# Odd heads of pairs 9 to 14: queries and keys from 7 block products in place of 8

## The chip, the cores and the metric

The kernel runs on one core of a Trainium2 chip. The metric is device time in microseconds (us) of one launch; the median of three runs of the kernel before is 1061.95 us.

## The reference, cut to what matters

```python
def _L0_attn_ref(hidden_states, Wq, bq, Wk, bk, Wv, bv, Wo, bo, gq, gk):
    q = hidden_states @ Wq + bq
    k = hidden_states @ Wk + bk
    v = hidden_states @ Wv + bv
    q = rms_norm(q, gq)
    k = rms_norm(k, gk)
    attn = softmax(q @ k.T / sqrt(128)) per head
    return (attn @ v) @ Wo + bo

x = x + _layernorm(_L0_attn_ref(_layernorm(x), ...))
x = x + _layernorm(_L0_ffn_ref(_layernorm(x), ...))
```

The input is 2 batches of 512 tokens, 512 wide; there are 32 heads of 128. The norm of queries and keys runs over all heads (4096 columns), so every query and key must be known before the first score.

## The kernel before, in words

Every float32 product is made of three float16 matmuls: each operand is split into a high half and a low half, and high x high, high x low and low x high are summed in PSUM (`three`, L1619). A stationary operand is 128x128, the moving one 512 columns.

**Phase A** (to about 330 us) computes queries and keys, head by head in 16 pairs of an even and an odd head (heads 2p and 2p+1 are pair p). TensorE's part is `q_or_k` (L1663): for a head four products, query and key (w = 0, 1) of batch 0 and of batch 1, each of 4 chunks x 3 = 12 matmuls of 512 columns. So a head is 48 matmuls. The even head writes PSUM banks 0 to 3, the odd one banks 4 to 7. The other engines' parts for a head:

- ScalarE (`phase_a`, L1198): the high halves of the weights of the head after next (`high_wa`), then per product the square (`square`, L1149, into `squares`), and for a query two copies with bias, the float32 one `q_s` (L1159) and its high half (L1161).
- GpSimd (`phase_a`, L762): for each batch the low half of the query (`low_q`, L747) and two additions of the squares to `acc` (`add_batch`, L753). After each head comes one more step, `more(par)`, which forms operands for block products of values: sums and differences of blocks of x, split into halves in `xs` (`high_a` to `split_g`, L796 to L837), 36 instructions in pairs 1 to 13 (L868 to L881).
- VectorE (`phase_a`, L2382): scale factors of the head after next (`next_factors`), its largest weight four heads ahead (`largest_qk`), the low halves of the weights (`low_wa`, L2219, two instructions of 512 columns with both tensors in SBUF), the key with bias and gain (`store_k`, L2324), and a reduction of one unit of the value or output weights (`largest_of_unit`).
- SyncE loads weights five heads ahead and stores query and key to DRAM.

Each engine's order is written out by hand; semaphores with running counts hold it together. In phase A TensorE waits for the low halves of the weights (`wa_lo_ready`) and for the key before in the same banks (`k_out_ready`), L1699 to L1710.

**Phase B** computes scores, softmax, values and outputs, pair by pair. Values of most pairs are already made there by the block scheme with 7 products (`product`, L1809), with the operands `xs` that GpSimd formed in phase A; SyncE waits for all 36 forms before it loads over their scratch `qk_in` (L577).

## Time and profile before

| what | us |
|---|---|
| runs | 1060.37, 1062.02, 1061.95 (median 1061.95) |
| the profiled execution, its own time | 1060.19 |
| its span | 1058.4 |
| TensorE busy | 1039.7 (98%) |
| VectorE busy | 828.2 (78%) |
| ScalarE busy | 764.0 (72%) |
| GpSimd busy | 763.4 (72%) |
| mean granted TensorE clock | 0.998 |

Busy time is what an engine spent in instructions, without the time in which it waited for a semaphore. 1.8 us of the profiled execution lie outside its span. A share over the whole span says little of phase A, whose third of the time has other loads than the rest; so the rows below are of stretches.

### The profile page before, as it was taken

What the parts mean: (1) busy time and instruction counts of PE and PEld (TensorE: products, weight loads), DVE (VectorE), ACT (ScalarE), POOL (GpSimd) and SP (SyncE); (2) the same over time, 40 slices, a digit from 0 to 9 for tenths busy, and PEclk for the clock granted to TensorE, in tenths of its full rate; (3) what the DMA queues carried; (4) which work ended last, traced back from release to release, by engine and by line L of the source; (5) the groups of instructions that cost most, each with busy time, mean ns of one, the idle gap of its engine ahead of it and who ended that gap; (6) DMA issues with size and microseconds to landing.
All of it is one profiled execution on the core that took longest, in us unless ns stands there. A gap on an engine that the chain in (4) does not pass through costs nothing.

```text
span 1058.4 us, 19677 instructions
## 1 busy us (share of the span) xinstructions
PE 1039.7 (98%) x5649; PEld 549.8 (52%) x5649; DVE 828.2 (78%) x1824; ACT 764.0 (72%) x1582; POOL 763.4 (72%) x717
## 2 busy tenths in 40 slices
PE   7999999999999999999999999999999999999997
PEld 4444444444444655556555555555555555555454
DVE  7777876667646778777887987888888888878887
ACT  4666766666647777776788787778787878877756
POOL 2687988788958577765777777778778778767313
PEclk9999999999999999999999999999999999999999
DMA  6678865656574569967667867876877987896702
GB/s 242 176 235 269 254 231 210 227 195 233 201 139 164 178 175 262 250 160 197 149 170 185 195 166 172 200 187 157 203 197 143 216 203 161 224 198 141 177 34 81
DMA packets 312761, 199.91 MB, mean 189 GB/s; under 512 B 275552, under 2 KB 279520, under 8 KB 312672
## 3 DMA queue, kind: packets, MB, share of 16 engines
q1 hardware_dynamic: 304752, 194.24, 68.1%
q10 hardware_dynamic: 7920, 4.62, 1.7%
q8 instruction: 39, 0.64, 0.2%
q14 instruction: 50, 0.41, 0.1%
HBM read 96.03 MB, written 35.68 MB: 124 GB/s over the span
## 4 chain that ended last, share of the span: by engine, by line
PE 87%; DVE 6%; ACT 3%; issue 1%; DMA 1%; POOL 1%; SPq 0%; DVEq 0%; ACTq 0%; POOLq 0%
PE ps L1621 26%; PE ps L1623 25%; PE ps L1622 25%; PE ps L1813 3%; PE ps L1814 3%; PE ps L1815 3%; ACT ps L1301 2%; DVE pair_q L2542 1%; ACT pair_q L1310 1%; DVE y L2555 1%; DMA pair_k<-pair_q 1%; DMA wa_stage<-w_qk 1%; DVE ps L2528 1%; DVE stats L2117 0%; PE ps L1733 0%
## 5 line engine op out<-in xcount | busy, mean ns | idle before, releaser
L1301 ACT ACTIVATE ps<-ps,neg_max 128x512 f32<-128x512 f32 x256 | 168.2, 657 | 57.7 <-DVE ps L2528 57.7
L2542 DVE SCALAR_TENSOR_TENSOR pair_q<-ps,row_inv,pair_q 128x512 f16<-128x512 f32 x256 | 174.2, 742 | 43.8 <-ACT pair_q L1310 40.4
L1621 PE MATMUL ps<-xh,wa_hi 128*128 128x512 f16 x512 | 194.1, 379 | 1.8 <-DVE wa_lo L2222 1.8
L1622 PE MATMUL ps<-xl,wa_hi 128*128 128x512 f16 x512 | 194.1, 379 | 0.0
L1623 PE MATMUL ps<-xh,wa_lo 128*128 128x512 f16 x512 | 194.1, 379 | 0.0
L2528 DVE TENSOR_SCALAR_CACHE_REDUCE ps<-ps,score_down 128x512 f32<-128x512 f32 x256 | 177.1, 753 | 15.2 <-PE ps L1623 14.5
L1310 ACT ACTIVATE pair_q<-ps,row_inv 128x512 f16<-128x512 f32 x256 | 154.5, 689 | 9.0 <-DVE row_inv L2535 8.8
L759 POOL TENSOR_TENSOR acc<-acc,squares 128x512 f32<-128x512 f32 x120 | 151.5, 1284 | 1.6 <-ACT squares L1152 1.6
L1152 ACT ACTIVATE squares<-ps,q_k_bias,qk_down 128x512 f32<-128x512 f32 x128 | 99.1, 785 | 42.9 <-PE ps L1623 28.6
L750 POOL TENSOR_TENSOR qk_out<-q_s,qk_out 128x512 f16<-128x512 f32 x64 | 75.5, 1181 | 52.4 <-ACT qk_out L1161 52.4
L2327 DVE TENSOR_SCALAR qk_out<-ps,k_b,k_g 128x512 f32<-128x512 f32 x64 | 51.8, 809 | 73.9 <-ACT squares L1152 73.8
L905 POOL TENSOR_TENSOR k_lo<-qk_in,k_hi 128x512 f16<-128x512 f32 x62 | 71.7, 1157 | 38.2 <-ACT k_hi L1258 38.1
L1621 PE MATMUL ps<-wo_hi,oth 128*128 128x512 f16 x256 | 97.1, 379 | 1.9 <-issue 0.9
L1621 PE MATMUL ps<-k_hi,qk_in 128*128 128x512 f16 x256 | 97.1, 379 | 1.2 <-issue 0.9
L1623 PE MATMUL ps<-wo_hi,otl 128*128 128x512 f16 x256 | 97.1, 379 | 0.0
L1622 PE MATMUL ps<-wo_lo,oth 128*128 128x512 f16 x256 | 97.1, 379 | 0.0
L1623 PE MATMUL ps<-k_hi,qk_in 128*128 128x512 f16 x256 | 97.1, 379 | 0.0
L1622 PE MATMUL ps<-k_lo,qk_in 128*128 128x512 f16 x256 | 97.0, 379 | 0.0
L1119 ACT ACTIVATE wa_hi<-wa_stage,qk_up 128x512 f16<-128x512 f32 x64 | 42.8, 718 | 75.0 <-DVE qk_up L2174 75.0
L936 POOL CAST oth<-o_t 128x512 f16<-128x512 f32 x62 | 38.3, 618 | 74.0 <-ACT o_t L1275 73.9
L1275 ACT ACTIVATE o_t<-ps,tab 128x512 f32<-128x512 f32 x62 | 42.7, 689 | 58.8 <-PE ps L1623 58.7
L1621 PEld LDWEIGHTS ps<-xh,wa_hi 128*128 128x128 f16 x512 | 50.3, 98 | 61.9 <-issue 2.1
(310 smaller groups left out, 2578.3 us busy)
## 6 DMA issues: line engine op xcount, KB each, us to landing
q_k_scratch<-qk_out SPq DMA_DIRECT2D x64, 512.0 KB, 4.0
qk_in<-q_k_scratch SPq DMA_DIRECT2D x64, 512.0 KB, 3.7
wa_stage<-w_qk SPq DMA_DIRECT2D x32, 512.0 KB, 4.2
u_stage<-w_vo SPq DMA_DIRECT2D x32, 512.0 KB, 5.3
wo_stage<-w_vo SPq DMA_DIRECT2D x16, 512.0 KB, 6.3
x_first<-w_vo SPq DMA_DIRECT2D x12, 512.0 KB, 4.4
qk_tops<-qk_top_scratch ACTq DMA_DIRECT2D x27, 128.0 KB, 3.5
pair_k<-pair_q SPq DMA_TRANSPOSE x130, 4.0
```

The lines of the kernel that those rows point to most:

```text
L750: pool.tensor_tensor(pair(qk_out[:, par, b, 1, :])[:, 1, :], q_s[:, par, b * S:(b + 1) * S], pair(qk_out[:, par, b, 1, :])[:, 0, :], ALU.s ...
L759: pool.tensor_tensor(acc[:, w, cols], acc[:, w, cols], squares[:, par, w, cols], ALU.add).then_inc(acc_ready, 1)
L905: pool.tensor_tensor(k_lo[:, s % 2, :], qk_in[:, s, 0, :], k_hi[:, s % 2, :], ALU.subtract).then_inc(qk_lo_ready, 1)
L1152: act.activation(squares[:, par, w, b * S:(b + 1) * S], ps[:, 4 * par + g, :], ACT.Square, bias=q_k_bias[:, par, w:w + 1], scale=qk_down[: ...
L1301: act.activation(ps[:, SCORE + i, :], ps[:, SCORE + i, :], ACT.Exp, bias=neg_max[:, sl, i:i + 1], scale=-1.0, accum_out=row_sum[:, sl, i:i ...
L1310: act.activation(pair_q[:, 0, i, :], ps[:, SCORE + i, :], ACT.Identity, scale=row_inv[:, sl, i:i + 1]).then_inc(high_ready, 1)
L1621: pe.matmul(outp, lhs[0], rhs[0], start=first, stop=False)
L1622: pe.matmul(outp, lhs[0], rhs[1], start=False, stop=False)
L1623: return pe.matmul(outp, lhs[1], rhs[0], start=False, stop=last)
L2327: dve.tensor_scalar(qk_out[:, par, b, 0, :], ps[:, 4 * par + 2 * b + 1, :], k_b[:, slot:slot + 1], k_g[:, slot:slot + 1], ALU.add, ALU.mul ...
L2528: dve.tensor_scalar(ps[:, SCORE + i, :], ps[:, SCORE + i, :], score_down[:, sl, i:i + 1], None, ALU.mult, ALU.min, accum_out=neg_max[:, sl ...
L2542: dve.scalar_tensor_tensor(out=pair_q[:, 1, i, :], in0=ps[:, SCORE + i, :], scalar=row_inv[:, sl, i:i + 1], in1=pair_q[:, 0, i, :], op0=AL ...
```

## The change

For six pairs (9 to 14) the odd head's query and key are no longer four products of 12 matmuls. Tokens are split into the first and the second 256 of each batch, the contraction into its first and last two chunks, the output into query and key: a product of 2x2 blocks, done with 7 block products (C, A, E, B, D, G, F) of 2 chunks x 3 = 6 matmuls of 512 columns. Four of the sums that the scheme wants are made by leaving products in PSUM and copying bank to bank.

- TensorE (`formed_pair`): the even head's four `q_or_k` with the odd head's block products between them, 90 matmuls for the pair. Before A it waits, in the first formed pair, for all forms of x (`x_formed` 30), in the others for the sums of queries before.
- GpSimd: the forms of x now stand in pairs 1 to 8, two after most heads (30 instructions). `formed_sums` adds and subtracts blocks of the next formed head's weights into `f_sum` (one instruction of 512 columns, three of 256), once between pairs 7 and 8 and then in pairs 9 to 13 after two additions. The low halves and additions of the odd head go by tokens.
- VectorE: forms the sums of G (six instructions `half_g` and `both_g`, in heads 7 to 12), adds saved C to the query banks (two instructions of 512 columns for a formed head), and splits the formed weights in `low_formed`: 512 columns that are used as they are and 1280 of sums.
- ScalarE: saves C with its bias, copies bank to bank three times for a formed head, squares the odd head's query from SBUF; `high_formed` has one instruction of 512 and one of 1280 columns.
- Both factors of a formed head become one (`next_factors(..., formed=True)`), since query and key weights are added.
- The pairs from 9 on are straight code on all engines; SyncE stores the odd head's two batches together at the pair's end.

Cut to its core:

```diff
@@ gpsimd
+            def formed_sums(h):
+                slot, f = h % 4, h // 2 - FIRST
+                pool.wait_ge(wa_loaded[slot], 16 * (h // 4 + 1))
+                if f > 0:
+                    pool.wait_ge(wa_lo_ready, 2 * h - 2)
+                w = wa_stage[:, slot]
+                pool.tensor_tensor(f_sum[:, 0:4 * P].rearrange("p (w c n) -> p w c n", w=2, c=2), w[:, :, 0:2, :],
+                                   w[:, :, 2:4, :], ALU.add).then_inc(w_formed, 1)
+                for k, one, other, op in ((F_E, w[:, 0, 0:2, :], w[:, 1, 2:4, :], ALU.add),
...
+                low_q(0, 0, 2 * h + 1)
+                add_one(1, -1, 0, 0, batch(0))
+                add_one(2, 0, 0, 1, batch(0))
+                if p < LAST_PAIR:
+                    formed_sums(h + 3)
+                add_one(3, 2, 1, 1, tokens(0))
...
-            phase_a(1, high_a)
-            phase_a(2, low_a)
-            phase_a(3, both_halves)
-            phase_a(4, split_a)
...
+            phase_a(1, high_a, low_a)
+            phase_a(2, both_halves, half(high_half, XA))
+            phase_a(3, half(low_half, XA), high_e)
+            phase_a(4, low_e, half(high_half, XE))
+            phase_a(5, half(low_half, XE), high_d)
+            phase_a(6, low_d, half(high_half, XD))
+            phase_a(7, half(low_half, XD), high_half_g)
+            formed_sums(2 * FIRST + 1)
+            phase_a(8, low_half_g)
+            for p in range(FIRST, LAST_PAIR + 1):
+                formed_pair(p)
@@ scalar
+            def high_formed(h):
+                slot, f = h % 4, h // 2 - FIRST
+                act.wait_ge(qk_up_ready, h + 1)
+                act.activation(corners(wa_hi[:, slot]), corners(wa_stage[:, slot]), ACT.Copy,
+                               scale=qk_up[:, slot, 0:1]).then_inc(wa_hi_ready, 1)
+                act.wait_ge(w_formed, 4 * f + 4)
+                act.activation(f_high[f % 2], f_sum, ACT.Copy,
+                               scale=qk_up[:, slot, 0:1]).then_inc(wa_hi_ready, 1)
@@ tensor
-            with pe.Fori(1, PAIRS // 2) as i:
+            with pe.Fori(1, PAIRS // 4 + 1) as i:
...
+                q_or_k(0, 0, slots[0])
+                pe.wait_ge(wa_lo_ready, 2 * h + 4)
+                pe.wait_ge(k_out_ready, 2 * h - 1)
+                product(W_C, C_BANK, True)
+                if f:
+                    pe.wait_ge(q_sum_ready, 2 * f)
+                else:
+                    pe.wait_ge(x_formed, X_FORMS)
+                product(W_A, Q_LAST, True)
+                q_or_k(0, 1, slots[0])
+                pe.wait_ge(v_copied, 4 * f + 2)
+                product(W_E, Q_LAST, False)
+                product(W_B, K_BANK, False)
+                q_or_k(0, 2, slots[0])
+                pe.wait_ge(v_copied, 4 * f + 3)
+                product(W_D, Q_LAST, False)
+                product(W_G, Q_FIRST, False)
+                q_or_k(0, 3, slots[0])
+                pe.wait_ge(v_copied, 4 * f + 4)
+                product(W_F, K_BANK, False)
@@ vector
+                dve.wait_ge(qk_product, products + 9)
+                for second, bank in enumerate((Q_FIRST, Q_LAST)):
+                    dve.wait_ge(v_copied, 4 * f + 3 + second)
+                    dve.scalar_tensor_tensor(out=over_tokens(q_s[:, 1, :], second), in0=by_half(ps[:, bank, :]),
+                                             scalar=Q_DOWN, in1=by_half(c_q), op0=ALU.mult,
+                                             op1=ALU.add).then_inc(q_sum_ready, 1)
+                if p < LAST_PAIR:
+                    low_formed(h + 3)
+                else:
+                    low_wa(h + 3, (h + 3) % 4)
+                dve.wait_ge(stored[0][1], 16 * p)
+                store_k(0, 1, slots[0], 8 * p + 6)
+                formed_key(1, 8 * p + 8)
```

How it moves instructions, at the two places that matter below. First GpSimd, from the odd head of pair 7 to the first formed pair. Before, the end of pair 7 and pair 8 (L750 is the low half of a query, L759 an addition of squares, L776 and L793 form and split x):

```order
L776 TENSOR_TENSOR xs<-qk_in,xs 128x512
L750 TENSOR_TENSOR qk_out<-q_s,qk_out 128x512
L759 TENSOR_TENSOR acc<-acc,squares 128x512 x2
L750 TENSOR_TENSOR qk_out<-q_s,qk_out 128x512
L759 TENSOR_TENSOR acc<-acc,squares 128x512 x2
L776 TENSOR_TENSOR qk_in<-xh,qk_in 128x512
```

Now the same place (L815 and L824 are the low half and the additions, L841 and L858 the forms of x, L902 and L907 the sums of weights):

```order
L841 TENSOR_TENSOR xs<-qk_in,xs 128x512
L858 CAST xs<-qk_in 128x512
L902 TENSOR_TENSOR w_sum<-wa_stage 128x512
L907 TENSOR_TENSOR w_sum<-wa_stage 128x256 x3
L815 TENSOR_TENSOR qk_out<-q_s,qk_out 128x512
L824 TENSOR_TENSOR acc<-acc,squares 128x512 x2
L815 TENSOR_TENSOR qk_out<-q_s,qk_out 128x512
L824 TENSOR_TENSOR acc<-acc,squares 128x512 x2
L841 TENSOR_TENSOR xs<-qk_in,xs 128x512
```

The sums of weights stand ahead of pair 8, and the last split of x, the one TensorE waits for, stands behind all of pair 8's additions.

Second VectorE, at the end of a formed pair (with the semaphores that each instruction waits for; L2748 adds C to the queries, L2495 and L2499 split the next formed head's weights, L2603 and L2725 write keys):

```order
L2748 SCALAR_TENSOR_TENSOR q_s<-ps,k_lo 128x2x256 [waits v_copied,qk_product]
L2748 SCALAR_TENSOR_TENSOR q_s<-ps,k_lo 128x2x256 [waits v_copied]
L2495 SCALAR_TENSOR_TENSOR wa_lo<-wa_stage,qk_up,wa_hi 128x2x256 [waits wa_hi_ready]
L2499 SCALAR_TENSOR_TENSOR rms_row<-w_sum,qk_up,rms_row 128x1280 [waits wa_hi_ready]
L2603 TENSOR_SCALAR qk_out<-ps,k_b,k_g 128x512 [waits sq_ready,stored0_1]
L2725 TENSOR_SCALAR qk_out<-ps,k_b,k_g 128x2x256 [waits sq_ready]
```

Both keys that end the pair now stand behind the split of 1280 columns, whose input comes from GpSimd by way of ScalarE. TensorE, at the start of the next pair, waits for them and for that split:

```order
L1820 MATMUL ps<-xh,wa_lo 128x512
L1939 MATMUL ps<-xh,w_form_a 128x512 [waits k_out_ready,wa_lo_ready]
L1940 MATMUL ps<-xl,w_form_a 128x512
L1941 MATMUL ps<-xh,w_form_a 128x512
L1939 MATMUL ps<-xh,w_form_a 128x512
L1940 MATMUL ps<-xl,w_form_a 128x512
L1941 MATMUL ps<-xh,w_form_a 128x512
L1939 MATMUL ps<-xs,wa_hi 128x512 [waits x_formed]
```

C (six matmuls) comes 12 matmuls into the pair, and in the first formed pair A stands 18 matmuls in, behind the wait for the forms of x.

## Rows read from the trace of the kernel before

**Rows 1.** The page: busy time, and slices of the span (tenths).
```profile
PE 1039.7 (98%) x5649; PEld 549.8 (52%) x5649; DVE 828.2 (78%) x1824; ACT 764.0 (72%) x1582; POOL 763.4 (72%) x717
PE   7999999999999999999999999999999999999997
POOL 2687988788958577765777777778778778767313
```

**Rows 2.** Windows in phase A: us, busy of each engine (instructions), PEclk, DMA share, GB/s.
```profile
100.00:140.00 40.00, 40.00 (x187) 18.16 (x186) 32.02 (x59) 28.47 (x49) 38.38 (x31) 1.00 0.84 273
225.00:245.00 20.00, 20.00 (x94) 9.10 (x93) 13.69 (x28) 13.01 (x22) 16.45 (x16) 1.00 0.57 208
```

**Rows 3.** Timeline, TensorE at 238 us: start us, us, instruction.
```profile
238.16 0.38 PE L1621 MATMUL ps<-xh,wa_hi 128*128 128x512 f16 x1
238.38 0.38 PE L1622 MATMUL ps<-xl,wa_hi 128*128 128x512 f16 x1
```

**Rows 4.** Timeline, ScalarE: squares that wait for a head's last product.
```profile
204.70 0.78 ACT L1152 ACTIVATE squares<-ps,q_k_bias,qk_down 128x512 f32<-128x512 f32 x1 [0.66 <-PE ps L1623]
...
215.06 0.78 ACT L1152 ACTIVATE squares<-ps,q_k_bias,qk_down 128x512 f32<-128x512 f32 x1 [0.66 <-PE ps L1623]
```

**Rows 5.** Timeline, GpSimd, heads 5 to 11, with idle time before and releaser.
```profile
81.40 1.16 POOL L750 TENSOR_TENSOR qk_out<-q_s,qk_out 128x512 f16<-128x512 f32 x1 [2.60 <-ACT qk_out L1161]
...
101.41 1.16 POOL L750 TENSOR_TENSOR qk_out<-q_s,qk_out 128x512 f16<-128x512 f32 x1 [1.56 <-ACT qk_out L1161]
102.52 2.49 POOL L759 TENSOR_TENSOR acc<-acc,squares 128x512 f32<-128x512 f32 x2
104.98 1.16 POOL L750 TENSOR_TENSOR qk_out<-q_s,qk_out 128x512 f16<-128x512 f32 x1
...
108.55 1.72 POOL L776 TENSOR_TENSOR qk_in<-qk_in 128x512 f32<-128x512 f32 x1
110.32 1.51 POOL L750 TENSOR_TENSOR qk_out<-q_s,qk_out 128x512 f16<-128x512 f32 x1
...
117.80 1.08 POOL L793 CAST xs<-qk_in 128x512 f16<-128x512 f32 x1
118.96 1.48 POOL L776 TENSOR_TENSOR xs<-qk_in,xs 128x512 f16<-128x512 f32 x1
120.40 1.16 POOL L750 TENSOR_TENSOR qk_out<-q_s,qk_out 128x512 f16<-128x512 f32 x1
...
130.16 1.16 POOL L750 TENSOR_TENSOR qk_out<-q_s,qk_out 128x512 f16<-128x512 f32 x1
...
138.88 1.61 POOL L750 TENSOR_TENSOR qk_out<-q_s,qk_out 128x512 f16<-128x512 f32 x1
```

**Rows 6.** Timeline, GpSimd, head 17.
```profile
200.95 1.16 POOL L750 TENSOR_TENSOR qk_out<-q_s,qk_out 128x512 f16<-128x512 f32 x1 [1.99 <-ACT qk_out L1161]
...
208.08 1.17 POOL L776 TENSOR_TENSOR qk_in<-xh,qk_in 128x512 f32<-128x512 f16 x1
```

**Rows 7.** Timeline, VectorE: the two splits of weights of one head.
```profile
108.06 2.76 DVE L2222 SCALAR_TENSOR_TENSOR wa_lo<-wa_stage,qk_up,wa_hi 128x512 f16<-128x512 f32 x2
```

**Rows 8.** By tile and by source: durations in ns, min/median/max.
```profile
L2222 DVE SCALAR_TENSOR_TENSOR wa_lo<-wa_stage,qk_up,wa_hi x64: 736/746/1754, 13.2 to 328.1; 128x512 f16<-128x512 f32 x64
L2542 DVE SCALAR_TENSOR_TENSOR pair_q<-ps,row_inv,pair_q x256: 732/741/752, 355.9 to 998.6; 128x512 f16<-128x512 f32 x128
```

**Rows 9.** Groups of GpSimd, 140 to 200 us: busy us, mean ns, idle before.
```profile
L750 POOL TENSOR_TENSOR qk_out<-q_s,qk_out 128x512 f16<-128x512 f32 x12 | 14.3, 1193 | 8.5 <-ACT qk_out L1161 8.5
L776 POOL TENSOR_TENSOR xs<-qk_in,xs 128x512 f16<-128x512 f32 x2 | 2.3, 1154 | 0.2
L793 POOL CAST xs<-qk_in 128x512 f16<-128x512 f32 x2 | 1.2, 616 | 0.0
```

**Rows 10.** Timeline, TensorE: first matmuls of constants, and the last matmul.
```profile
1.76 5.30 PE L1634 MATMUL ps<-ones,ident 128*128 128x256 f16 x24 [1.76 <-POOL ident L727]
...
10.84 1.47 PE L1634 MATMUL ps<-ones,ident 128*128 128x256 f16 x12
...
1050.83 0.27 PE L1623 MATMUL ps<-bt_hi,hw_lo 128*128 128x256 f16 x1
```

**Rows 11.** Windows behind the last matmul, columns as in rows 2.
```profile
1052.00:1054.00 2.00, 0.00 (x0) 0.00 (x0) 1.93 (x4) 0.11 (x1) 2.00 (x2) 1.00 0.10 38
1054.00:1056.00 2.00, 0.00 (x0) 0.00 (x0) 1.84 (x5) 0.00 (x0) 0.61 (x2) 0.72 0.95 355
1056.00:1058.40 2.40, 0.00 (x0) 0.00 (x0) 0.00 (x0) 0.00 (x0) 0.00 (x0) 0.50 0.29 109
```

**Rows 12.** Waits, 100 to 325 us: us in total, times, longest.
```profile
DVE qk_most L2207 <- DMA qk_tops<-qk_top_scratch: 8.4, 2, 7.4
```

396 lines of the change are left out of this document (312 added, 84 removed).

## The prediction

> **What bounds the kernel now.** Read the page's busy times first [rows 1]: TensorE is busy in 98% of the span and in nine tenths or more of every slice but the first and the last. The windows of phase A say the same in its middle, 20.00 of 20.00 us at full clock, while VectorE, ScalarE and GpSimd have a fifth to a third of their time free there [rows 2]. So a matmul less is time less, as long as nobody makes TensorE wait. Consecutive matmuls of 512 columns start 0.216 us apart [rows 3] (the 0.38 us of a row is latency). Last products of successive heads end 10.36 us apart [rows 4], which is 48 x 0.216; a pair takes 20.7 us.
>
> The second thing to see is GpSimd. From 100 to 140 us it was busy 38.4 of 40 us [rows 2], with a load that is small by its own durations: two low halves and four additions, which take 7.14 us when nothing disturbs them (2 x (1.11 + 2.46), from the starts at 101.41, 102.52 and 104.98 [rows 5]), and one or two forms of x of 0.6 to 1.2 us [rows 9]. What fills the rest are forms that took 1.72, 1.08 and 1.48 us [rows 5]. They lie where VectorE splits weights: the pair of splits at 108.06 took 2.76 us in place of 2 x 0.74 [rows 7, 8]. The two engines take turns. A split of 512 columns costs GpSimd about 0.45 us (1.72 against 1.27), and VectorE waits for a whole GpSimd instruction. An instruction with one tensor in PSUM, L2542, does not suffer: 732 to 752 ns over 256 of them, though GpSimd works beside it [rows 8].
>
> **Removed.** 6 odd heads go from 48 to 42 matmuls: 36 x 0.216 = **7.8 us less**. That the matmuls do go is certain: the changed order has 36 fewer. ScalarE and VectorE get more to do but fit: ScalarE was busy 13.0 of 20 us [rows 2], so 13.5 in a pair, and gains four copies and the 1280 columns and loses two query copies and the two halves of another head's weights, about 15 of the 19.4 us of a formed pair (90 x 0.216). VectorE goes from 14.2 to about 16.5 us, and waits for GpSimd on top. I cost their load itself at nothing; if that cover fails it shows in the pace below.
>
> **The wait for the forms of x.** The first formed pair starts at 204.5 (the square at 204.70 begins 0.2 after the product's end [rows 4]). A is wanted 18 matmuls later, at 208.4. It needs the last split of x, which stands behind all additions of head 17. Were GpSimd on time, as it is before, the form at 208.08 would end at 209.25 [rows 6]: a wait of 0.9 us at the least.
>
> It won't be on time. At 101.41 it has just caught up with ScalarE (idle 1.56 us before), and so it would now, since the one more form in each of the heads before is covered by idle time such as the 2.60 and the 1.56 [rows 5]. From there to the low half of head 17 at 200.95 [rows 6] are 99.5 us for heads 7 to 16. A head with a cast and a two-input form was measured in the continuous stretch, turns with VectorE included: 10.08 and 9.76 (110.32 to 120.40 to 130.16), and one with a single form 8.72 (130.16 to 138.88) [rows 5]. Two two-input forms are 0.5 more than cast and form. So heads 7, 10, 11: 3 x 10.4; heads 8, 9, 12 to 15: 6 x 9.9; head 16: 8.8; the sums of weights between pairs 7 and 8: one of 512 columns at 1.23 and three of 256 at half that and a little, 0.67, together 3.2. Sum 102.6, **3.1 us late**. VectorE's six instructions for G have both tensors in SBUF and take their turns too, 6 x 0.45 = 2.7 if all hit a busy GpSimd, and head 17 itself has 0.9 of turns that the on-time head 17 did not have. The wait is 0.9 + 3.1 = 4.0 us at one end and 7.6 at the other. I take **6.5**, near the upper end, since a GpSimd without idle time leaves no place to miss it.
>
> **The clock.** The last matmul starts at 1050.83 [rows 10]; the granted clock is whole until 1054, 0.72 in the next 2 us and 0.50 after [rows 11]. TensorE had been idle for about 4 us when it fell to 1.2 GHz. At the start, 24 matmuls of 256 columns took 5.30 us, later 12 took 1.47 [rows 10], so a restart runs at half speed for up to 5.3 us and loses up to 2.6. An idle time of 6.5 us probably brings that. Bounds 0 and 2.6, I take **1.8**; a wait of 4 us may bring none.
>
> **The pace of the formed pairs.** GpSimd's work in one: 4 low halves x 1.11, 8 additions x 1.23, 3.2 for the next sums: 17.5 us. Turns: three splits of 512 columns x 0.45 and one of 1280, whose hold I scale by columns from what a 512 split takes once its turn has come (the pair ended at 110.82, 0.55 after the form that ended at 110.27 [rows 5, 7]): 1.4. That makes 20.2 against TensorE's 19.4. GpSimd falls behind by 0.8 a pair, and there is no store to live on: the sums go to ScalarE, to VectorE's split of 1280 columns, and behind it stand both keys that the next pair waits for. In the first formed pair the long wait lets GpSimd catch up, so the starts of pairs 11 to 14 pay: 4 x 0.8, and a little for a chain over three engines, **4.0**. Bounds: nothing, if TensorE still sets the pace; 4 x 1.9 = 7.6 with the longer hold below. The sums' 0.67 has no row; a whole 1.23 each would add 1.7 a pair, nothing for three would take 2.0 off. The Trainium skill (GPSIMD Engine Reference, Elementwise — side-by-side cycle accounting) gives 4.497 us for a two-input instruction of 2048 columns; an estimate from it is 0.56 for 256 and its own dispatch beside that, and by 0.56 alone the sum would be about 1 us lower.
>
> **Sum.** -7.8 + 6.5 + 1.8 + 4.0 = **+4.5**. Against the profiled execution's own 1060.2 us that is 1064.7; the median of the runs is 1.8 above that execution, so 1066.5. About 0.2%, 2 us, is what a measurement of this kernel can tell from no change.
>
> **Rivals.**
>
> *B, GpSimd keeps up: faster.* The place is the last split of x. If the turns cost GpSimd less because its instructions and VectorE's fall apart, as they do later in phase A of the kernel before, where it is idle 2 us a head [rows 6], ten heads fit in 99.5 us; the point is 3.1 us, 0.3 a head. Then the wait is 0.9, without a fall of the clock: -7.8 + 0.9 + 4.0 = -2.9, 1059.0; with TensorE setting the pace too, -6.9. For it: my 3.1 is 3% of 102.6. Against it: the heads were measured, not summed, and none of the new instructions has idle time to go to.
>
> *C, the hold is longer.* A split holds GpSimd off for its whole duration, 0.74, and for 1280 columns 1.56 (768 more at 0.55 per 512). Then the pace is 17.5 + 3 x 0.74 + 1.56 = 21.3, 1.9 over TensorE's, 7.6 for four starts, and the wait is at its upper end: -7.8 + 7.6 + 1.8 + 7.6 = +9.2, 1071.2. Against it: 1.72 is 0.45 over 1.27, not 0.74 [rows 5]. [...] That they exclude each other the trace shows; by its numbers the exclusion is shorter than the instruction.
>
> *D, small costs cancel.* The wait at its lower end, no fall of the clock, pace 4.0: -7.8 + 4.0 + 4.0 = +0.2, 1062.2.
>
> A late load of factors like the one of 7.4 us [rows 12], which now would stand ahead of a key that the pair waits for, can add up to 7 us; it was one in 225 us, and I only widen the range for it.
>
> **How the numbers follow.** The forecast gets 0.45, C 0.17, B 0.25, D 0.13. Faster 0.25 is B, the same 0.13 is D, slower 0.62 the other two. The range leaves out the better half of B below (a tenth) and the last of C with a late load above: 1058 to 1072. The slower cases alone lie between 1064 and 1072.
>
> **What would show it.** Right: 36 fewer matmuls; one TensorE wait of 4 to 8 us at L1939 near 208, put down to GpSimd's L841; GpSimd without idle time from 100 to 215; PEclk below 1.00 behind it; starts of pairs 20.0 to 20.8 us apart from pair 11 on, with waits at L1939 put down to VectorE's L2603 or L2499. Wrong: a wait near 1 us there (B), starts 19.4 apart (TensorE sets the pace), or 21 and more (C). If GpSimd is on time and still the pairs are long, the cause is a chain that I haven't priced.

## The result, and the profile after

The changed kernel takes 1074.2 us in the median (1070.74 to 1075.03, four runs), the kernel before 1061.99 beside it (1060.37 to 1063.5): ratio 1.0109, 95% interval 1.0082 to 1.0136, 12.2 us slower. The forecast was 1066.5: the sign is right, the time lies outside the range, which ended at 1072. The profiled execution took 1073.9 us, its span is 1072.1.

The page of the changed kernel, to be read beside [rows 1]: busy times and the slices in tenths.

```profile
PE 1037.5 (97%) x5613; PEld 548.0 (51%) x5613; DVE 867.6 (81%) x1848; ACT 771.2 (72%) x1594; POOL 796.6 (74%) x735
PE   8999999799989999999999999999999999999997
PEclk9999999989999999999999999999999999999999
POOL 2699999979988557776678778768778778767313
```

The 36 matmuls are gone (5649 to 5613). Two slices of TensorE are no longer nines, and GpSimd is at nine tenths or more from the third slice to the eleventh, but for the ninth, where it stood idle for 4.91 us behind TensorE's long wait. Where the 13.7 us of span went, from the starts of matmuls in both traces (score products are counted from 0):

| stretch | before, us | after, us | difference |
|---|---|---|---|
| start to first score product (phase A) | 350.12 | 360.16 | +10.04 |
| to the 128th score product | 336.70 | 336.70 | 0.0 |
| 128th to the 192nd | 161.17 | 164.99 | +3.8 |
| to the end | 210.40 | 210.24 | -0.2 |

TensorE's waits at L1939 in phase A, from the timeline. In brackets stand the idle time and what ended it; each wait is 0.16 us longer than its bracket, since a matmul's 0.38 is 0.16 longer than the step of 0.216.

```profile
216.77 0.61 PE L1939 MATMUL ps<-xs,wa_hi 128*128 128x512 f16 x1 [8.08 <-POOL xs L841]
...
256.87 0.38 PE L1939 MATMUL ps<-xh,w_form_a 128*128 128x512 f16 x1 [0.21 <-DVE qk_out L2603]
...
296.33 0.38 PE L1939 MATMUL ps<-xh,w_form_a 128*128 128x512 f16 x1 [0.45 <-DVE qk_out L2603]
...
320.74 0.59 PE L1939 MATMUL ps<-xh,rms_row 128*128 128x512 f16 x1 [4.83 <-DVE qk_out L2603]
```

And windows behind the two long ones (columns as in [rows 2]):

```profile
211.00:216.00 5.00, 0.00 (x0) 0.00 (x0) 1.01 (x1) 0.00 (x0) 5.00 (x5) 0.50 0.83 271
216.00:222.00 6.00, 5.23 (x15) 1.96 (x16) 1.15 (x2) 1.82 (x3) 3.05 (x3) 0.57 0.39 146
222.00:226.00 4.00, 4.00 (x20) 1.83 (x19) 3.26 (x6) 1.65 (x3) 2.04 (x2) 1.00 0.08 32
...
320.00:324.00 4.00, 3.26 (x9) 1.24 (x10) 2.75 (x10) 3.51 (x8) 4.00 (x4) 0.57 0.51 152
```

In the idle time the granted clock fell to half (1.2 GHz), and when TensorE resumed it kept that for some microseconds: from the matmul at 216.77 to the one 18 later, at 222.83, are 6.06 us, 2.2 more than 18 x 0.216, and from 320.74 to the one 24 later, at 327.31, 6.57 us, 1.4 more. So phase A: -7.8 (36 matmuls) + 8.2 + 2.2 (wait for the forms of x and its clock) + 1.0 (two small waits) + 5.0 + 1.4 (the wait at 320.74) = +10.0, which is all of it.

The first wait is GpSimd's. Timeline of GpSimd, heads 16 and 17, against [rows 6]:

```profile
198.45 1.16 POOL L815 TENSOR_TENSOR qk_out<-q_s,qk_out 128x512 f16<-128x512 f32 x1
199.56 4.26 POOL L824 TENSOR_TENSOR acc<-acc,squares 128x512 f32<-128x512 f32 x2
...
208.47 1.14 POOL L815 TENSOR_TENSOR qk_out<-q_s,qk_out 128x512 f16<-128x512 f32 x1
...
215.57 1.14 POOL L841 TENSOR_TENSOR xs<-qk_in,xs 128x512 f16<-128x512 f32 x1
```

Head 17's low half begins 7.5 us later than before (208.47, 200.95), where I had 3.1. Head 7 began 0.9 later (102.28, 101.41), and heads 7 to 16 took 106.2 us with the sums of weights, not 102.6; GpSimd was busy 99.16 us of 100 to 200. What grew are instructions beside VectorE's splits and forms of G: a pair of additions took 2.94 or 3.4 us again and again, where it takes 2.49 undisturbed, and once 4.26, beside the splits of 512 and 1280 columns. Behind the long wait GpSimd was idle:

```profile
223.96 1.27 POOL L918 TENSOR_TENSOR acc<-acc,squares 128x512 f32<-128x512 f32 x1 [4.91 <-ACT squares L1257]
```

The last wait is a load's. VectorE at the end of pair 13, then SyncE's issues:

```profile
313.84 1.22 DVE L2412 TENSOR_REDUCE qk_top<-wa_stage 128x2 f32<-128x1024 f32 x1 [4.12 <-DMA wa_stage<-w_qk]
315.33 1.22 DVE L2611 TENSOR_REDUCE vo_top<-u_stage 128x1 f32<-128x1024 f32 x1 [0.27 <-DMA u_stage<-w_vo]
316.47 1.28 DVE L2748 SCALAR_TENSOR_TENSOR q_s<-ps,k_lo 128x512 f32<-128x512 f32 x2
...
318.32 1.55 DVE L2499 SCALAR_TENSOR_TENSOR rms_row<-w_sum,qk_up,rms_row 128x1280 f16<-128x1280 f32 x1
```

```profile
300.11 0.82 SPq L621 DMA_DIRECT2D q_k_scratch<-qk_out  x2
300.99 0.71 SPq L627 DMA_DIRECT2D vo_top_scratch<-top_v  x1
301.74 1.14 SPq L511 DMA_DIRECT2D wa_stage<-w_qk  x1
```

The reduction over head 31's weights waited for their load, and query sums, splits and keys stand behind it on VectorE. The load was issued behind a store of 128 partitions of 4 bytes (`top_v`, the largest value weight) and landed some 12 us later. The kernel before has the same order: the small store was issued at 290.00, the load at 290.38, and both took 9.5 us to land (such a load took 3.9 in the median there), but nobody waited for it. The 7.4 us of [rows 12] are of the same time, a wait at 306.98, but for maxima that ScalarE loads back in its own queue; TensorE did not wait behind it, and no run shows that the small store caused it.

In phase B there is one more, which no part of my sum had. VectorE, four alike instructions of one step shortly behind the point where the loop of four pairs jumps back:

```profile
700.14 0.75 DVE L2877 TENSOR_SCALAR_CACHE_REDUCE ps<-ps,score_down 128x512 f32<-128x512 f32 x1
700.82 0.14 DVE L2877 DVE_READ_ACCUMULATOR ps<-ps,score_down 128x1 f32 x1
703.73 0.76 DVE L2877 TENSOR_SCALAR_CACHE_REDUCE ps<-ps,score_down 128x512 f32<-128x512 f32 x1 [2.77 <-issue]
```

"issue" is time in which it waited for nothing that the profile shows. Between the second and the third of these rows VectorE stood for 2.77 us.

### The profile page after: what moved, and what is told of

Its sections match the earlier page's. It is cut to its first block, busy times and chain, and to the rows that moved or that the text cites. A ratio compares the mean times of both kernels' runs of the same rounds, so it can differ in the third digit from the quotient of the medians.

```text
span 1072.1 us, 19041 instructions
## 1 busy us (share of the span) xinstructions
PE 1037.5 (97%) x5613; PEld 548.0 (51%) x5613; DVE 867.6 (81%) x1848; ACT 771.2 (72%) x1594; POOL 796.6 (74%) x735
## 4 chain that ended last, share of the span: by engine, by line
PE 75%; DVE 9%; ACT 5%; POOL 4%; issue 4%; DMA 3%; SPq 1%; ACTq 0%; DVEq 0%; POOLq 0%
PE ps L1818 21%; PE ps L1820 21%; PE ps L1819 21%; PE ps L2067 3%; PE ps L2069 3%; PE ps L2068 3%; ACT ps L1498 2%; DVE pair_q L2891 2%; POOL acc L824 1%; PE ps L1939 1%; DMA u_stage<-w_vo 1%; PE ps L1941 1%; PE ps L1940 1%; DMA pair_k<-pair_q 1%; ACT pair_q L1507 1%
## 5 line engine op out<-in xcount | busy, mean ns | idle before, releaser
L1818 PE MATMUL ps<-xh,wa_hi 128*128 128x512 f16 x416 | 158.2, 380 | 0.4 <-DVE wa_lo L2487 0.4
L1819 PE MATMUL ps<-xl,wa_hi 128*128 128x512 f16 x416 | 158.0, 380 | 0.0
L1820 PE MATMUL ps<-xh,wa_lo 128*128 128x512 f16 x416 | 157.9, 380 | 0.0
L1257 ACT ACTIVATE squares<-ps,q_k_bias,qk_down 128x512 f32<-128x512 f32 x104 | 80.0, 786 | 45.1 <-PE ps L1820 34.3
L824 POOL TENSOR_TENSOR acc<-acc,squares 128x512 f32<-128x512 f32 x72 | 100.5, 1416 | 1.6 <-ACT squares L1257 1.6
L1004 POOL TENSOR_TENSOR qk_in<-qk_in,rms_row 128x512 f32<-128x512 f32 x62 | 78.9, 1272 | 0.6 <-ACT rms_row L1460 0.6
L2487 DVE SCALAR_TENSOR_TENSOR wa_lo<-wa_stage,qk_up,wa_hi 128x512 f16<-128x512 f32 x52 | 65.2, 1292 | 14.8 <-ACT wa_hi L1224 14.7
L1043 POOL TENSOR_TENSOR otl<-o_t,oth 128x512 f16<-128x512 f32 x62 | 71.6, 1155 | 5.0
L815 POOL TENSOR_TENSOR qk_out<-q_s,qk_out 128x512 f16<-128x512 f32 x52 | 64.4, 1240 | 13.8 <-ACT qk_out L1266 13.7
```

The source lines that it names most:

```text
L824: pool.tensor_tensor(acc[:, w, cols], acc[:, w, cols], squares[:, par, w, cols], ALU.add).then_inc(acc_ready, 1)
L1004: pool.tensor_tensor(qk_in[:, s, 0, :], qk_in[:, s, 0, :], factors(b), ALU.mult).then_inc(qk_scaled, 1)
L1043: pool.tensor_tensor(otl[:, sl, cols], o_t[:, sl, :], oth[:, sl, cols], ALU.subtract).then_inc(otl_ready, 1)
L1257: act.activation(squares[:, par, w, b * S:(b + 1) * S], ps[:, 4 * par + g, :], ACT.Square, bias=q_k_bias[:, par, w:w + 1], scale=qk_down[: ...
L1818: pe.matmul(outp, lhs[0], rhs[0], start=first, stop=False)
L1819: pe.matmul(outp, lhs[0], rhs[1], start=False, stop=False)
```

## The experiments

All are against the kernel before on the same chip; 1.0109 is the changed kernel. "Starts" are the distances between first matmuls of C from pair 9 to pair 14, 19.4 us where TensorE sets the pace (90 x 0.216); the changed kernel had 29.8, 19.8, 19.4, 20.0, 24.4.

### The deadline of the forms of x, alone

```diff
-                    pe.wait_ge(x_formed, X_FORMS)
+                    pe.wait_ge(x_formed, X_FORMS - 2)
                 product(W_A, Q_LAST, True)
...
+                if not f:
+                    pe.wait_ge(x_formed, X_FORMS)
                 product(W_G, Q_FIRST, False)
```

> TensorE waits before A only for 28 forms of x (all that A, E and D read), and for the last two (the low half of G's operand) before G, 48 matmuls later. In the changed kernel the one wait for all 30 took 8.24 us and about 2.2 us of half clock behind it. Theory 1, the wait is only a deadline put too early: both go, 10.4 us less than the changed kernel, about 1.0011 of the kernel before, and TensorE's idle time at 208 to 217 us is under 0.5 us. Theory 2, GpSimd's lateness is real and is paid later: it still ends its last form near 216.7, its weight sums of pair 9 end near 224, ScalarE and VectorE need about 4 us more, and C of pair 10, wanted near 226.5, waits 1 to 4 us; after it GpSimd, whose pair takes 20.2 us, has no time to catch up, 0.8 us a pair for four pairs: 4 to 6 us less than the changed kernel, 1.005 to 1.007, with the waits at L1939 spread over pairs 10 to 14. I hold theory 2 for likelier.

Measured 1.0064 (1.0051 to 1.0077), 1068.07 us: theory 2. The wait at 208 is gone, and the next pair starts late:

```profile
223.57 0.39 PE L1939 MATMUL ps<-xh,w_form_a 128*128 128x512 f16 x1 [0.16 <-ACT ps L1350]
...
231.22 0.59 PE L1939 MATMUL ps<-xh,rms_row 128*128 128x512 f16 x1 [3.60 <-DVE qk_out L2605]
```

Starts 23.5, 22.0, 19.6, 21.3, 23.1. About 10 us were taken away and about 5 came back: the wait was a backlog, and in the changed kernel it was also what let GpSimd catch up.

### The small store and the load behind it

Three runs. In the first only the store moves, ahead of pair 9, with VectorE's reduction before it; in the second only the load moves, ahead of the odd head's store (and so of the small one); the third has both and the split wait.

```diff
+            sp.wait_ge(v_top_ready, 1)
+            sp.dma_start(vo_top_scratch[0], top_v[:, :]).then_inc(v_top_stored, 16)
             for p in range(FIRST, LAST_PAIR - 1):
                 formed_pair(p)
-            sp.wait_ge(v_top_ready, 1)
-            sp.dma_start(vo_top_scratch[0], top_v[:, :]).then_inc(v_top_stored, 16)
```

> The store of the largest value weight (128 partitions of 4 bytes) and the reduction before it stand ahead of pair 9 and not between pairs 12 and 13. In the changed kernel that store was issued at 300.99 us, 0.75 us ahead of the load of head 31's weights, which took 11.8 us and led to TensorE's wait of 4.99 us at 320.7 and half clock behind it. Theory 1, the small store slows the load: the wait at 320.7 goes, 6.4 us less, 1.005. Theory 2, the load is issued too late in any case, because the odd head's store stands ahead of it in SyncE's queue and waits for GpSimd, and the landing of 7 to 12 us varies with what else moves: the wait shrinks by the 0.9 us that the store held the queue, or not at all, 1.009 to 1.011. Theory 3, a chance delay of transfers: gone or not whatever is done; the store alone changes nothing.

1.0098 (1.0085 to 1.0112). The wait of 4.12 us for weights at 313 shrank to 0.64, but new ones came behind the store's new place: products were late by 2.1 and 0.9 us at 234.8 and 239.6. There VectorE waited for no weights, though the load behind the store took 10.0 us. It was ScalarE that stood, for its own small store of maxima, issued 6.2 us behind SyncE's, and TensorE waited for ScalarE's bank copy:

```profile
232.34 0.78 ACT L1257 ACTIVATE squares<-ps,q_k_bias,qk_down 128x512 f32<-128x512 f32 x1 [6.35 <-DMA qk_top_scratch<-qk_top]
```

Moving the store moved the cost.

```diff
-                weights(h)
+                if p == FIRST:
+                    weights(h)
...
                              qk_out[:, 0, 1]).then_inc(stored[0][1], 16)
+                if p < LAST_PAIR:
+                    weights(h + 2)
                 sp.wait_ge(k_out_ready, 2 * h + 4)
```

> SyncE issues the load of the next odd head's weights ahead of the odd head's store (which waits for GpSimd's last low half of queries) and not behind it; the store of the largest value weight stands behind that load too. In the changed kernel that load was issued 4 to 5 us after it could. Theory 2 of the wait at 320.7 (the load is issued too late): the wait goes, 6.4 us less than the changed kernel, 1.005, and no reduction of weights waits for a load in pairs 10 to 14. Theory 3 (chance): one of the loads may still be late by more than the 4 us won, and the time stays at 1.010. Theory 1 (the small store): also gone here, since the load is now ahead of the store; the run with the store moved alone tells the two apart.

1.0113 (1.0098 to 1.0128): no gain, though no reduction of weights waited in pairs 10 to 14 and the load near 298, now ahead of the small store, landed in 5.8 us. The odd head's first key now waited for the odd head's store (1.86, 1.57, 2.73 us), which stood behind the load. The same few microseconds, on another transfer.

> The split wait, the early store and the early load together. If the three are independent and the wait of 8.24 us only a deadline: 10.4 and 6.4 us less than the changed kernel, -4.6 us against the kernel before, 0.9957. If GpSimd's lateness is paid later: 4 to 6 us and 6.4 us less, 0.999 to 1.001; then GpSimd has no idle time from 100 to 320 us and the waits at L1939 are put down to the splits of formed weights.

1.0064 (1.0051 to 1.0077): neither number, no better than the split wait alone. The store now stood at the first formed pair, and there VectorE waited 5.02 us for weights and TensorE 6.0.

Since transfers were late behind the store in both places, the suspected cost was multiplied: the same 512 bytes stored five times, each right ahead of a load.

```diff
                 formed_pair(p)
+                sp.wait_ge(v_top_stored, 16 * (p - FIRST + 1))
+                sp.dma_start(vo_top_scratch[0], top_v[:, :]).then_inc(v_top_stored, 16)
```

> The run with the early store, and the small store (128 partitions of 4 bytes, the same numbers again) is repeated behind pairs 9, 10, 11 and 12, each time right ahead of the load of an odd head's weights: five in all. In every run where it stood right ahead of that load, VectorE waited 3.0 to 5.0 us for the weights in that pair. Theory S, the small store delays the load behind it: such a wait appears in each of pairs 10 to 13, 3 to 6 us at each start of the next pair, 12 to 20 us more than with one store, 1.021 to 1.030. Theory B, it is the burst of a store and two loads of 512 KB each, in which the small one changes little: under 4 us more, 1.010 to 1.014.

1.0329 (1.0314 to 1.0343), 1096.78 us: 24.6 us more than with one store, 6 us for each. VectorE's waits for weights:

```profile
257.08 1.22 DVE L2414 TENSOR_REDUCE qk_top<-wa_stage 128x2 f32<-128x1024 f32 x1 [4.97 <-DMA wa_stage<-w_qk]
...
283.16 1.22 DVE L2414 TENSOR_REDUCE qk_top<-wa_stage 128x2 f32<-128x1024 f32 x1 [1.62 <-DMA wa_stage<-w_qk]
...
309.48 1.22 DVE L2414 TENSOR_REDUCE qk_top<-wa_stage 128x2 f32<-128x1024 f32 x1 [6.06 <-DMA wa_stage<-w_qk]
```

From issue to landing, median over 225 to 330 us, the changed kernel and this one:

```profile
wa_stage<-w_qk SPq DMA_DIRECT2D x8, 512.0 KB, 7.7
```

```profile
wa_stage<-w_qk SPq DMA_DIRECT2D x8, 512.0 KB, 12.2
```

That the small store delays what is issued behind it is shown by these runs. (The expectation says that VectorE waited for the weights in every run with the store ahead of the load; with the store early and nothing else it did not, as said above, and with the split wait alone it waited 3.11 us for a store instead.) Is it the place in the queue? Five again, from ScalarE's queue at the pairs' starts:

```diff
             for p in range(FIRST, LAST_PAIR + 1):
+                if p < LAST_PAIR:
+                    if p > FIRST:
+                        act.wait_ge(v_top_stored, 16 * (p - FIRST))
+                    act.dma_start(vo_top_scratch[0], top_v[:, :]).then_inc(v_top_stored, 16)
                 formed_pair(p)
```

> The run with five small stores, but each is issued by ScalarE, at the start of pairs 9 to 13, in ScalarE's own DMA queue and not in SyncE's ahead of the load of weights. Five in SyncE's queue made 1.0329 (the same run with one: 1.0098). ScalarE stores 128 partitions of 8 bytes in its queue in every head, and those landed in 3.5 us in the middle. Theory queue: what delays the load is that it stands behind the small store in one queue: no wait for weights of more than 3 us in pairs 10 to 13, 1.006 to 1.012. Rival, the small store itself disturbs the transfers of all queues (128 writes of 4 bytes to one line of memory): 1.025 or more here too.

1.0169 (1.0147 to 1.0191): between the two. No wait for weights in pairs 10 to 13, but keys waited in every pair for the odd head's store:

```profile
252.26 0.81 DVE L2728 TENSOR_SCALAR qk_out<-ps,k_b,k_g 128x512 f32<-128x512 f32 x1 [2.51 <-DMA q_k_scratch<-qk_out]
...
274.23 0.81 DVE L2728 TENSOR_SCALAR qk_out<-ps,k_b,k_g 128x512 f32<-128x512 f32 x1 [2.54 <-DMA q_k_scratch<-qk_out]
```

So five cost 7.6 us over the run with one there, in place of 24.6. That is put down to the queue, but not shown by itself: ScalarE's stores were also issued some 5 to 8 us before SyncE's load and not right ahead of it, and a run in SyncE's queue at that time wasn't made. What is shown is that a part reaches the other queue: stores of queries and keys took 8.2 us to land in the median, 5.2 in the changed kernel, and the loads of weights 9.9, not 7.7. The Trainium skill (DMA: Bandwidth & Descriptors, Queues, rings and completion order) says that a transfer's completion count is written only after every earlier write of that DMA engine, across its queues; that would couple them, but no run here shows the mechanism.

### GpSimd's backlog

The eight copies to float16 of the forms of x go from GpSimd to ScalarE, one head later each.

```diff
-                pool.tensor_copy(two(xs[:, 0, kind, c, :]), src).then_inc(x_formed, 1)
...
+                act.wait_ge(x_formed, count)
...
+                act.activation(by_half(xs[:, 0, kind, c, :]), by_half(qk_in[:, 2 if kind == XG else 0, c, :]),
+                               ACT.Copy).then_inc(x_formed, 1)
```

> The changed kernel with the eight high halves of the forms of x made by ScalarE, nothing else. For the wait of 8.24 us before A: my account says it is GpSimd's backlog, so that every microsecond taken from GpSimd between 60 and 210 us comes off it: 8 x 0.65 = 5.2 us and the turns with VectorE that these casts took: the wait is 1.5 to 3 us, with no fall of the clock behind it (2.2 us), while the wait of 4.99 us at 320 stays: 7 to 8.5 us less than the changed kernel, 1.003 to 1.0045. Rival, GpSimd is held by waits for squares and copies of ScalarE, which now has more to do: the wait stays over 5 us, 1.008 or more.

1.0063 (1.0045 to 1.0081), between the two. The trace is of the slowest of its five executions (1075.3 us, the median is 1070.2). The wait fell from 8.08 to 5.29 us, by half of what was taken off, since GpSimd now twice waited for ScalarE:

```profile
195.92 1.16 POOL L815 TENSOR_TENSOR qk_out<-q_s,qk_out 128x512 f16<-128x512 f32 x1 [0.64 <-ACT qk_out L1265]
...
206.61 1.15 POOL L815 TENSOR_TENSOR qk_out<-q_s,qk_out 128x512 f16<-128x512 f32 x1 [2.40 <-ACT qk_out L1265]
```

With all three edits of above:

> The run with all three changes, and the eight high halves of the forms of x are made by ScalarE (copies to float16) and no more by GpSimd. That takes about 8 x 0.65 = 5.2 us from GpSimd between 60 and 200 us. In the run with all three changes TensorE's idle time in the formed pairs is still 10.3 us, 6.03 of it at the start of pair 10. Theory G, GpSimd's lateness is what the formed pairs pay for: its last form ends 5 to 7 us earlier, all waits at the starts of pairs shrink, phase A is 5 to 7 us shorter, 1.000 to 1.002. Theory L, the wait at pair 10 is that for a load (VectorE waited 5.02 us for the weights at 225.12, with the query sums and the splits behind it): GpSimd is earlier, but a wait of 3 to 6 us stays there, 1.003 to 1.006.

1.0017 (1.0008 to 1.0026), 5 us less than without the copies: theory G by the time, though in the two traces phase A is only 3.6 us shorter. The wait of 6.0 us at the start of pair 10 was gone; in its place F of pair 9 waited 3.0 us for ScalarE, which stood for 7.21 us. Its own small store of maxima, issued 2.5 us behind `top_v`'s, took 12.2 us to land.

### The order on VectorE

```diff
                 formed_key(0, 8 * p + 3)
-                top(h + 1)
-                unit(h + 3)
...
                 formed_key(1, 8 * p + 8)
+                top(h + 1)
+                unit(h + 3)
```

> The run with ScalarE's copies, and in VectorE's formed pair the two reductions over loads (the largest weight of a head four later and the largest of a unit) stand behind both keys, at the pair's end, and not ahead of the query sums; ScalarE stores and loads the largest weights correspondingly later. Theory L: no wait for a load can hold the sums, the splits or the keys any more, sums come 2.4 us earlier in each pair, the waits at the starts of pairs fall below 1 us together, 0.995 to 0.998. Rival: the factors of the next odd head are now late (stored maxima land and come back in 8 to 10 us), VectorE waits for them in the middle of each pair, and each pair is longer than 19.4 us by 1 to 2 us: 1.003 or more. Theory G alone: no change against the run with ScalarE's copies.

(ScalarE's stores and loads of the maxima move with them.) 1.0148 (1.013 to 1.0166): the rival. The weights' reduction starts the chain of factors, and put last it makes them late: TensorE had ten waits at L1953, the longest 3.87, 3.80 and 2.97 us, and VectorE up to 3.90 us for the maxima.

Only the unit's reduction last, and the small store one pair earlier still (ahead of head 16):

> The run with the split wait, the early load and ScalarE's copies, with two edits: the small store and the reduction before it stand ahead of head 16, one pair before the formed pairs (not at their start), and VectorE's reduction of one unit (1.13 us) stands behind both keys and not ahead of the query sums. In the run with ScalarE's copies the waits at the starts of formed pairs were 2.98, 1.87, 0.75 and 0.75 us. Theory chain: each pair ends with query sums, splits and keys one behind the other on VectorE, so what is taken from ahead of them comes off every start: the three smaller waits go or fall to under 0.8, and the first goes with the store (there ScalarE waited 7.21 us, held by its own load of maxima behind a store that took 12.2 us): phase A is 4 to 6 us shorter than before, 0.996 to 0.998 in all. Rival, GpSimd's 20.2 us a pair sets the pace by now (TensorE needs 19.4): the waits stay near 0.8 a pair, 0.999 to 1.001.

0.9999 (0.999 to 1.0008): the rival again. No wait is long any more, but the starts are 21.5, 20.2, 20.8, 20.2, 20.5.

> The same without the early load: the next odd head's weights are loaded behind the odd head's store again. Alone the early load changed nothing: it took the wait for weights away, but the store behind it landed later and the odd head's first key waited for it by 1.6 to 2.7 us. Theory, both orders cost alike: within 0.2% of the run with the early load. Rival, with GpSimd relieved the load is in time anyway and the store's lateness remains the only cost: 0.1 to 0.2% faster than with the early load.

1.0002 (0.999 to 1.0015): both orders cost alike.

> The run with the unit's reduction last, and in each formed pair the eighth addition of squares covers 16 columns and not 512: the squares of keys of the odd heads' second tokens are left out of the norm in six pairs, so 1.2 us a pair less for GpSimd and nothing else changed. In that run C's products of pairs 10 to 14 started 20.2, 20.8, 20.2 and 20.5 us apart, which is GpSimd's 20.2 us and not TensorE's 19.4. Theory GpSimd's pace: with 19.0 us GpSimd is faster than TensorE, the pairs start 19.4 to 19.6 apart and phase A is 3 to 4.5 us shorter, 0.996 to 0.997. Rival, the chain of sums, splits and keys on VectorE sets the pace (VectorE is busy 17.8 to 18.7 of 20 us): the pairs stay at 20.2 or fall by 0.2 at most, 0.999 to 1.000.

This kernel leaves out the squares of keys that are named above. 1.0009 (0.9997 to 1.0022): no gain, so the time doesn't bear the theory out. The profiled execution, one of the slowest of its twelve, does in part: starts 25.2, 19.4, 21.3, 19.4, 22.6. Two pairs reached 19.4, which none of the pairs had in the run it comes from. In the others ScalarE was held:

```profile
309.21 0.78 ACT L1260 ACTIVATE squares<-ps,q_k_bias,qk_down 128x512 f32<-128x512 f32 x1 [6.51 <-DMA qk_top_scratch<-qk_top]
```

It waits in its own queue until its store of maxima has landed, to load them back, and bank copies stand behind.

### Instructions that come late

```diff
                 h, par = 4 * i + o, o % 2
+                if h > 5:
+                    for _ in range(4):
+                        dve.sem_inc(begun, 1)
```

> The changed kernel with four more semaphore increments ahead of each of VectorE's heads from 6 on, in straight code; nothing else. It is for the 3.6 us that the changed kernel loses in phase B, between the 128th and 192nd score product, 164.99 us against 161.17 before, all near 697 to 707 us, where a loop of four pairs jumps back, and near 849. There VectorE sat idle 2.77 us at L2877 with nothing that it waited for, in the middle of four alike instructions. Theory C, instructions came late: where the idle time falls hangs on where the loop lies in the instruction stream, so moving VectorE's loop by some 40 instructions changes it: that stretch takes 161 to 163 us in this run or in the one with twice as many, and the place of the idle time moves. Rival: it is a wait for data that the profile doesn't name (counts or buffers changed by the formed pairs): 165 us in both.

1.0108 (1.0093 to 1.0124), as without them.

> The same with eight semaphore increments ahead of each of VectorE's heads from 6 on. Theory C: the stretch between the 128th and 192nd score product differs from 165 us here or in the run with four, and VectorE's idle time without a releaser stands at another instruction. Rival: 165 us in both. Phase A may be up to 1 us longer by the increments themselves.

1.011 (1.0094 to 1.0125). The stretch took 163.02 and 161.90 us (164.99), and VectorE's idle time without releaser is in neither. The waits without releaser between 690 and 712 us, first the changed kernel, then the one with eight:

```profile
DVE ps L2877 <- issue: 2.8, 1, 2.8
PEld ps L1818 <- issue: 1.1, 1, 1.1
PEld ps L2068 <- issue: 0.9, 1, 0.9
PE ps L2068 <- issue: 0.7, 1, 0.7
PE ps L1818 <- issue: 0.7, 1, 0.7
```

```profile
PEld ps L1818 <- issue: 1.4, 1, 1.4
PEld ps L2068 <- issue: 1.0, 1, 1.0
PE ps L1818 <- issue: 0.9, 1, 0.9
PE ps L2068 <- issue: 0.7, 1, 0.7
```

All traces agree. In the 13 of the changed kernel and its variants without increments VectorE stands at this line for 2.2 to 2.9 us without a releaser, and the stretch takes 163.2 to 165.0 us; in the six with increments it does not, and the stretch takes 161.9 to 163.0. (Single pairs of traces don't tell: with the split wait alone it took 163.42.) Empty increments can't supply data, so VectorE's instructions came late; why, no run shows. What the increments win is in the traces alone: the medians of these two hardly differ from 1.0109. On the run with the unit last:

> The run with the unit's reduction last, and four more semaphore increments ahead of each of VectorE's heads from 6 on, as in the run that shortened the stretch from the 128th to the 192nd score product from 164.99 to 163.02 us. Theory C (instructions late after the loop's jump back): 1 to 2 us less than without them, that stretch 161.5 to 163 us, and no idle time without releaser on VectorE there; in all 0.995 to 0.997. Rival: the increments cost VectorE in phase A what they save, no difference.

0.9985 (0.9972 to 0.9997), less than the theory's 0.995 to 0.997; its interval overlaps that of 0.9999. VectorE's idle time there is gone.

> The run with the unit's reduction last and eight semaphore increments ahead of each of VectorE's heads from 6 on, in place of four (which gave 0.9985) or none (0.9999). In the two runs of the changed kernel with increments, the stretch from the 128th to the 192nd score product took 163.02 us with four and 161.90 with eight, 164.99 with none. If the place of the loop in the instruction stream is what counts: that stretch 161.2 to 162.2 us, 0.997 to 0.9985. Rival: what is left there is TensorE's own late instructions, and eight do nothing that four did not: 0.9985 to 0.9995.

0.9994 (0.9983 to 1.0005): the rival. The stretch took 162.41 us, 162.19 with four and 163.17 with none. TensorE's own part stays.

### ScalarE's wait for its own store

```diff
                 square_key(0, 6)
-                if p < LAST_PAIR:
-                    load_tops(h + 4, 0)
...
                     high_formed(h + 3)
+                    load_tops(h + 4, 0)
```

> The run with the unit's reduction last and four increments (0.9985), and in each formed pair ScalarE issues the load of the next even head's largest weights behind its copies of the formed weights, and not ahead of the squares of the third product. ScalarE waits in its own queue until its small store of these maxima has landed, and in the run with seven additions that held it for 6.51 us (squares at 309.21), with F of pair 13 waiting 2.28 us for the bank copy behind it. Theory: such a landing of 6 to 12 us is now covered: F's waits (0.43 to 1.56 us in the run with four increments) go, pairs start 20.2 us apart everywhere (GpSimd's pace), 1 to 3 us less, 0.996 to 0.998. Rival: the factors come too late now, VectorE waits for the maxima at the start of the next pair, and a pair is longer by 1 to 2 us: 1.002 or more.

0.9953 (0.9939 to 0.9966), 1056.24 us: the theory, and a little below its 0.996. F waits in no pair any more, but the starts are 19.4, 19.4, 20.2, 20.9, 21.4 and not 20.2 everywhere.

> The same without the early load of the odd head's weights: it stands behind the odd head's store again. With ScalarE no longer held, what is left of waits for transfers is the odd head's key behind its store (up to 2.2 us with the early load) or the weights (with the late one). Theory: the store in time is worth more, since each odd store frees the key of the next pair: the same or 0.1% faster than with the early load. Rival: 0.1 to 0.3% slower, as weights come late again.

0.9957 (0.9943 to 0.9971), 1056.0 us: alike. These two beat both kernels, the first by 4.6 us against the median of before beside it. In the second the starts are 19.4, 20.2, 20.1, 20.2, 20.2 and the windows are even (columns as in [rows 2]):

```profile
225.00:245.00 20.00, 20.00 (x94) 9.00 (x93) 18.49 (x32) 14.56 (x25) 20.00 (x17) 1.00 0.75 223
245.00:265.00 20.00, 19.42 (x91) 8.65 (x90) 18.77 (x32) 14.59 (x25) 20.00 (x17) 1.00 0.76 224
265.00:285.00 20.00, 19.43 (x91) 8.72 (x90) 18.25 (x32) 14.60 (x25) 20.00 (x17) 1.00 0.81 222
```

with TensorE's only waits there at the starts of pairs 11 to 14, the first and the last of them:

```profile
247.08 0.38 PE L1947 MATMUL ps<-xh,w_form_a 128*128 128x512 f16 x1 [0.58 <-DVE qk_out L2613]
...
307.56 0.38 PE L1947 MATMUL ps<-xh,rms_row 128*128 128x512 f16 x1 [0.58 <-DVE qk_out L2613]
```

GpSimd has no idle time in these windows (20.00 of 20.00), and each of four starts is 0.74 us late.

## Why the prediction was wrong, step by step

- **Removed, 7.8 us.** Right: 36 matmuls fewer. ScalarE's and VectorE's load I had costed at nothing; what counted was not their load but their order.
- **The wait for the forms of x, 6.5 within 4.0 to 7.6.** The place, the releaser and the mechanism are right (L1939 near 208, GpSimd's L841, no idle time before); put at 6.5, it was 8.2. The step that failed in this term is "3 x 10.4, 6 x 9.9, 8.8", heads measured in the kernel before and carried over: heads 7 to 11 took 10.3 to 11.2 us, where VectorE's forms of G stand, and head 16 10.0 and not 8.8.
- **The clock, 1.8 within 0 to 2.6.** 2.2 us behind that wait; 1.4 more behind a wait I did not forecast.
- **The pace, 4.0.** GpSimd's pace is as I had it: in the changed kernel its weight sums begin at 225.19, 246.20, 266.35, 286.74 and 306.93, the last four 20.15, 20.39 and 20.19 apart, against 20.2. Three sums of 256 columns took 2.1 us together, 0.7 each, where I had 0.67. The estimate of 0.56 from the Trainium skill (GPSIMD Engine Reference, Elementwise — side-by-side cycle accounting), with a dispatch beside it, is not far off. Rival C's 21.3 is refuted: a split of 512 columns held an addition off by 0.45 us (2.94 against 2.49), not by its own 0.74. The Trainium skill (SBUF — State Buffer, Who interferes with whom) says of a VectorE instruction with two inputs in SBUF only that it contends with a GpSimd instruction that reads SBUF, and the trace agrees; the hold for a whole instruction it states for VectorE's 2-port modes. But TensorE paid only 1.0: behind the long wait GpSimd had been idle 4.91 us, most likely a store that 0.8 a pair drew on, so "there is no store to live on" was wrong for this execution; where the waits were removed (the run with the load back and later maxima), the four starts cost 4 x 0.74 = 3.0, near my 4 x 0.8.
- **The late load, "can add up to 7 us; I only widen the range for it".** This is the largest step that failed: 5.0 + 1.4 us that the sum put at nothing. I took one event in 225 us for chance. Before, it came shortly behind `top_v`'s store and the load that follows it, which both took 9.5 us; the changed kernel issues them in the same order, among formed pairs that do wait for the load. The four runs with the store in this place and the load behind it had the wait (4.12, 4.26, 3.01 and 4.33 us for weights); with the split wait alone it fell on a key, 3.11 us for its store. I had read the wait, and not what was issued around it.
- **Phase B, nothing.** It cost 3.8 us in the profiled execution. That straight code in place of a loop moves the next loop in each engine's instruction stream, and that this can cost anything, was in no term. Either of the two terms that were missing was enough to leave the range: 1074.2 less 6.4 is 1067.8, less 3.8 it is 1070.4, and both lie inside. Some 1.7 us of the 3.8 go with VectorE's late instructions (the stretch is 163.9 us in the mean of the 13 traces without increments, 162.2 in the six with them); the rest is not accounted for.
- **Rivals B and D** needed a wait of 0.9 or 4.0 us at the first A; it was 8.2.
- Sum by the measured terms: -7.8 + 8.2 + 2.2 + 1.0 + 6.4 + 3.8 = 13.8, against 13.7 of span. Without the two missing terms it would be +3.6, near the 4.5 that I had, but by two errors that nearly cancel: the pace cost 3.0 less and the wait with its clock 2.1 more.

What stays open: how the small store delays transfers, in its own queue and in the other, how much of that is the queue and how much the time of its issue, and what sets where an engine's instructions come late (only VectorE's part was moved; TensorE's wasn't tried). That GpSimd alone sets the last 0.8 us a pair rests on its full windows and on two pairs of one execution.

## What to carry to other kernels

When all engines of a stage wait for each other once a pass, price the order and not the load: taking 10 us of wait away brought 5, and each removed wait showed the next holder (forms, a load, a store, a queue that waits for its own transfer, and at last GpSimd's real 20.2 us). A rare long wait in the trace is a question to the queue in front of it before it is called chance; repeating the suspect several times can answer it in one run. And an engine should not wait in its queue for a small store of its own to land, when the load behind it can stand later.

## What was unexpected of the hardware

- A store of 128 x 4 bytes right ahead of a load of 512 KB cost about 6 us of kernel time each, in SyncE's queue (24.6 us for four more), and took 9 to 12 us to land itself. The load behind it landed in 9 to 12 us, ahead of it in 5.8. ScalarE's stores of 128 x 8 bytes land in about 4 us in the median, but near it one took 12.2.
- Shortly behind a loop's jump back VectorE stood for 2.2 to 2.9 us in the midst of a step, in 13 traces, with nothing that it waited for; four or eight empty instructions in each of twelve heads ahead of the loop removed that in all six traces that have them.
- A split of 512 columns on VectorE, both inputs in SBUF, took 0.74 us and held GpSimd's additions off by 0.45.
- After an idle time of 8.1 us TensorE ran at half clock to 221.2, 4.4 us after it resumed, and lost 2.2 us; after one of 4.8 us it did so for 2.9 us and lost 1.4.
